# Projection, norm, first routing and its dispatch of a graph and mixture-of-experts kernel put into one block that works by groups of tiles

## What is computed

```python
# graph attention, its last lines: hidden is [2048, 512]
hidden = hidden @ W_out + b_out
x = x + elu(hidden)
# first mixture of experts, on the layer norm of x
h = layernorm(x)
p = softmax(h @ gate_w)                      # 8 experts
w, sel = top_k(p, 2); w = w / w.sum(-1)      # two experts per token
g, u = h @ w_gate[e], h @ w_up[e]            # [512, 384] each
y = (silu(g) * u) @ w_down[e]                # [384, 512]
x = x + sum over the two chosen experts of w * y
```

## Time and profile before

| | us |
|---|---|
| median of 3 runs | 2196.76 (2195.17 to 2202.2) |
| the profiled execution | 2201.98 |
| its span | 2200.2 |
| mean granted TensorE clock | 0.949 |

### The profile page before, as it was taken

The page is one execution under the profiler, slowest core; times in us unless marked ns, Lnnn a source line. Parts: engine busy times, 40 slices in busy tenths (PEclk is TensorE's granted clock), DMA queues, the critical chain, the costliest instruction groups (busy, mean ns, idle before and its releaser), DMA issues. The chain is left out here.

```text
span 2200.2 us, 38541 instructions
## 1 busy us (share of the span) xinstructions
PE 1950.8 (89%) x15937; PEld 1714.8 (78%) x15941; DVE 1280.7 (58%) x1732; ACT 1101.2 (50%) x1182; POOL 468.4 (21%) x335
## 2 busy tenths in 40 slices
PE   4869999999987169999948979949999999999998
PEld 4859999999965069999936857638888888888886
DVE  7799988888656347777758033533434334344342
ACT  4699888886934135555412033224435344253441
POOL 2033222211120422222225401262101011011011
PEclk9979999999989679999979989969999999999999
DMA  6443333323202558888757322253334344353432
GB/s 249 155 164 122 117 108 122 117 83 31 98 6 77 196 183 252 250 250 250 186 168 257 122 77 77 75 150 121 103 119 133 98 134 128 106 138 93 125 104 109
DMA packets 154248, 300.01 MB, mean 136 GB/s; under 512 B 16091, under 2 KB 53083, under 8 KB 149968
## 3 DMA queue, kind: packets, MB, share of 16 engines
q1 hardware_dynamic: 135792, 262.30, 36.9%
q0 software_dynamic: 18336, 35.98, 7.7%
HBM read 227.23 MB, written 79.71 MB: 140 GB/s over the span
## 5 line engine op out<-in xcount | busy, mean ns | idle before, releaser
L823 PE MATMUL attn_acc<-heads_vals,gat_adj 128*128 128x99 bf16 x2048 | 284.6, 209 | 0.0
L2093 DVE TENSOR_TENSOR moe_w_lo<-moe_raw,moe_w_hi 128x2048 fp32r<-128x2048 f32 x64 | 146.8, 2293 | 234.6 <-ACT moe_w_hi L2050 234.6
L821 PE MATMUL attn_acc<-heads_vals,one_x 128*128 128x99 bf16 (+1 forms) x2048 | 240.9, 231 | 18.6 <-DVE one_x L735 13.2
L821 PE MATMUL attn_acc<-heads_vals,heads_mask 128*128 128x99 bf16 (+1 forms) x2048 | 238.5, 229 | 0.0
L2050 ACT CAST moe_w_hi<-moe_raw 128x2048 fp32r<-128x2048 f32 x64 | 122.2, 1909 | 207.8 <-PE moe_y_ps L2018 192.6
L688 ACT ACTIVATE heads_mask<-gat_s_row,heads_big_s 128x2048 fp8e4<-128x2048 f32 x104 | 197.8, 1989 | 35.3 <-PE attn_acc L823 35.3
L821 PEld LDWEIGHTS attn_acc<-heads_vals,one_x 128*128 128x128 fp8e4 x2048 | 197.9, 99 | 15.7 <-issue 15.3
L823 PE MATMUL attn_acc<-heads_vals,attn_below 128*128 128x99 bf16 x2048 | 204.9, 212 | 5.3 <-issue 5.3
L688 ACT ACTIVATE one_x<-gat_s_row,heads_big_s 128x2048 fp8e4<-128x2048 f32 x101 | 192.1, 1989 | 23.5 <-PE attn_acc L823 23.5
L821 PEld LDWEIGHTS attn_acc<-heads_vals,heads_mask 128*128 128x128 fp8e4 x2048 | 197.3, 98 | 5.5 <-issue 5.4
L201 PE MATMUL moe_h_ps<-moe_x_hi,moe_w_hi 128*128 128x512 f32 x512 | 200.1, 391 | 1.6 <-DVE moe_x_lo L2098 1.6
(11 more groups left out here) (347 smaller groups left out, 4736.2 us busy)
## 6 DMA issues: line engine op xcount, KB each, us to landing
moe_raw<-in_L_ffn_W_dram SPq DMA_DIRECT2D x64, 1024.0 KB, 5.2
moe_wg<-in_L_ffn_w_gate_dram SPq DMA_DIRECT2D x23, 768.0 KB, 9.1
moe_wu<-in_L_ffn_w_up_dram SPq DMA_DIRECT2D x23, 768.0 KB, 10.7
moe_wd<-in_L_ffn_w_down_dram SPq DMA_DIRECT2D x23, 768.0 KB, 12.3
gat_s_row<-s_rows SPq DMA_DIRECT2D x16, 1024.0 KB, 6.4
sym_a<-in_adj_dram SPq DMA_DIRECT2D x32, 512.0 KB, 4.3
one_seq<-sent SPq DMA_DIRECT2D x23, 514.0 KB, 3.6
sent<-all_zeros SPq DMA_DIRECT2D x10, 1028.0 KB
```

The costliest lines, as they stand in the source:

```text
L821: mm = pe.matmul(o[:, 0:first], mask[u][:, j, cols], both[:, 0:first], start=(j == 0 and b % 2 == 0), stop=(j == NT - 1), skip_group_check ...
L823: mm = pe.matmul(o[:, 3 * C1:6 * C1], second, both[:, 3 * C1:6 * C1], start=False, stop=(j == NT - 1), skip_group_check=True)
L2093: dve.tensor_tensor(w_lo[n % 2][:], raw[:, n % R], w_hi[n % 2][:], ALU.subtract).then_inc(w_low, 1)
```

## The change

`norm_stats`, `route` and `dispatch_labelled` go; `project_out` becomes `project_route`, one block that holds the projection, the norm, the routing and all 32 indirect transfers. The 16 tiles are taken in five groups (`PASSED`: 4, 4, 4, 2, 2). The main loop has 19 steps; step s multiplies tile s and lets each engine do, at places written out by hand (three per step), the routing work of a group some steps back. The normalizing moves from DVE to ACT and is done twice, into `wide` for the first choice and into a spare region for the second, so that the two copies of a row carry their own weight. The two-buffer `rT_ps` of the routing becomes one buffer, the three-buffer `xT` two.

A token's row in the table no longer depends on the counts of all 16 tiles: expert e owns rows 2048 e and following. So a group can be sent when it is counted. The table grows from 5888 rows to 18176 and is still cleared in whole. The first row of each block of 256 is worked out at the end (`block_row`) and read by SP into a register ahead of each load of rows. The blocks of experts wait for nothing: SP loads rows, then weights.

The diff, cut to its core (setup of tiles and semaphores and the unchanged functions are left out):

```diff
+PASSED = [slice(0, 4), slice(4, 8), slice(8, 12), slice(12, 14), slice(14, 16)]
+PLACES = 3
+PASSED_TURN = [16, 28, 40, 46, 52]
+PASSED_SCORE = [21, 33, 45, 49, 54]
+PASSED_BACK = [22, 34, 46, 50, 55]
+PASSED_RANK = [25, 37, 49, 53, 56]
+CHOOSE_IN = [7, 11, 15, 17, 18]
+PLACE_IN = [8, 12, 16, 17, 18]
+STEPS = NT + 3
...
             def _(pool):
...
+                def send(g, q):
+                    pool.wait_ge(placed, g + 1)
+                    for n in members(PASSED[g]):
+                        row = second(slice(n, n + 1)) if q else wide[:, n:n + 1, 0:ROW]
+                        pool.indirect_dma_start(out=table, ...
...
+                for t in range(NT):
+                    divide(t)
+                    if t == NT - 4:
+                        send(0, 0)
+                    if t == NT - 3:
+                        send(0, 1)
+                for g in range(1, NG):
+                    for q in range(TOPK):
+                        send(g, q)
+                pool.wait_ge(put, SENT)
...
             def _(act):
...
+                for s in range(STEPS):
+                    for g in range(NG):
+                        if s == PASSED[g].stop + 1:
+                            take_root(g)
+                    if 0 <= s - 1 < NT:
+                        exponential(s - 1)
+                    if s + 2 < NT:
+                        high_part(s + 2)
+                    for g in range(NG):
+                        if s == PASSED[g].stop + 1:
+                            normalize(g)
+                    for at in range(PLACES * s, PLACES * s + PLACES):
+                        for g in range(NG):
+                            n = PASSED[g].start + at - PASSED_TURN[g]
+                            if at == PASSED_RANK[g]:
+                                take_tail(g)
+                            if at == PASSED_SCORE[g]:
+                                keep_scores(g)
+                            if n in members(PASSED[g]):
+                                keep_turned(n)
+                    for g in range(NG):
+                        if s == PASSED[g].stop + (2 if g < NG - 1 else 1):
+                            normalize_second(g)
...
             def _(dve):
...
+                for s in range(STEPS):
+                    for g in range(NG):
+                        if s == PASSED[g].stop + 1:
+                            scale(g)
+                    if 0 <= s - 1 < NT:
+                        finish(s - 1)
+                    if s + 2 < NT:
+                        low_part(s + 2)
+                    if 0 <= s - 1 < NT:
+                        take_stats(s - 1)
+                    for g in range(NG):
+                        if s == PASSED[g].stop:
+                            take_variance(g)
+                    for g in range(NG):
+                        if s == CHOOSE_IN[g]:
+                            choose(g)
+                        if s == PLACE_IN[g]:
+                            place(g)
...
             def _(pe):
...
+                def turn_row(n):
+                    pe.wait_ge(normed, n + 1)
+                    if n:
+                        pe.wait_ge(r_copied, n)
...
+                def beside(at):
+                    for g in range(NG):
+                        n = PASSED[g].start + at - PASSED_TURN[g]
+                        if at == PASSED_RANK[g]:
+                            rank(g)
+                        if at == PASSED_BACK[g]:
+                            turn_back(g)
+                        if at == PASSED_SCORE[g]:
+                            score(g)
+                        if n in members(PASSED[g]):
+                            turn_row(n)
...
+                pe.wait_ge(w_loaded, 16)
+                pe.wait_ge(counted, 1)
+                for s in range(STEPS):
+                    if s + 2 < NT:
+                        turn(s + 2)
+                    beside(PLACES * s)
+                    if s < NT:
+                        multiply(s, (0, 1))
+                    beside(PLACES * s + 1)
+                    if s < NT:
+                        multiply(s, (2, 3))
+                    beside(PLACES * s + 2)
...
                 def load_rows(p, r):
+                    row = sp.value_load(block_row[0:1, bass.ds(p, 1)], min_val=0, max_val=table.shape[0] - BR)
                     sp.dma_start(x[:, SB * r:SB * r + SB, :],
-                                 table[bass.ds(p * BR, BR), :].rearrange("(s q) d -> q s d", q=P)).then_inc(x_in[r], 16)
+                                 table[bass.ds(row, BR), :].rearrange("(s q) d -> q s d", q=P)).then_inc(x_in[r], 16)
...
+                load_rows(0, 0)
                 load_weights(0, 0)
+                load_rows(1, 1)
                 load_weights(1, 1)
-                for q in range(TOPK):
-                    for g in range(4):
-                        sp.wait_ge(put[q][g], 64)
-                load_rows(0, 0)
-                load_rows(1, 1)
...
-    rows0, rows1 = NB0 * BR, E * CAP
+    rows0, rows1 = E * N + (NB0 - N * TOPK // BR) * BR, E * CAP
```

More of the change, by code:

```diff
@@ new lines, in project_route @@
+        cmp = c.sb("cmp", [P, E, N // BR])
+        count, blocks, ends = c.sb("count", [P, 1, E]), c.sb("blocks", [P, 1, E]), c.sb("ends", [P, E + 1])
+        cmpb, owned = c.sb("cmpb", [P, NB0, E]), c.sb("owned", [P, NB0, E])
+        blk, skipped, row_at = (c.sb(n, [P, NB0]) for n in ("blk", "skipped", "row_at"))
+        xT = [c.ps(f"xT{u}", [P, KD, P]) for u in range(2)]
+        out = [c.ps(f"out{u}", [P, D]) for u in range(R)]
+        rT_ps = c.ps("rT_ps", [P, KD, P])
+        lgT_ps = c.ps("lgT_ps", [E, G, P])
@@ L901, in project_out, with second, seconds @@
+        put = c.sem("put")
+        def second(tiles):
+            if tiles.start == NT - 1:
+                return last[:]
+            assert tiles.stop < NT
+            return spare[:, ROW * tiles.start:ROW * tiles.stop].rearrange("p (t w) -> p t w", w=ROW)
+        def seconds(g):
+            tiles = PASSED[g]
+            if tiles.stop < NT:
+                return [tiles]
+            return [slice(tiles.start, NT - 1), slice(NT - 1, NT)]
         with nc.Block() as block:
@@ new lines, in scale, with spread @@
+                def scale(g):
+                    tiles = PASSED[g]
+                    dve.wait_ge(rooted, g + 1)
+                    newton_rsqrt(ch, rstd[:, tiles], root[:, tiles], var[:, tiles], tn[:, tiles])
+                    dve.scalar_tensor_tensor(out=shift[:, tiles], in0=mv[:, tiles, 0], scalar=-1.0, in1=rstd[:, tiles],
+                                             op0=ALU.mult, op1=ALU.mult).then_inc(scaled, 1)
+                def spread(row, n):
+                    return row.rearrange("p (a e) -> p a e", a=1).to_broadcast([P, n, E])
@@ new lines, in rank @@
+                def rank(g):
+                    pe.wait_ge(chosen_s, g + 1)
+                    tiles = PASSED[g]
+                    pe.matmul(rank_ps[:, tiles, :], k.before[:], sel[:, tiles, :], start=True, stop=True)
+                    pe.matmul(total_ps[:, tiles, :], k.ones[:], sel[:, tiles, :], start=True, stop=True).then_inc(ranked, 1)
+                def beside(at):
[9 more added lines that the diff above has]
+                            turn_row(n)
```

464 lines of the change are left out of this document (200 added, 264 removed).

## The result

The changed kernel takes 2187.89 us (median of 18 runs, 2183.93 to 2193.89) beside 2198.68 us of the kernel before (18 runs, 2193.53 to 2204.3): the difference of the medians is 10.8 us. The ratio, taken from the runs side by side, is 0.9958, 95% interval 0.995 to 0.9966, so 0.42% faster, about 9.2 us. The profiled execution spans 2190.9 us in place of 2200.2. All medians here are over undisturbed executions; two of the ten of `e3_root_later`, at 3068 and 4640 us, are left out.

The account below looks back on a forecast made before the run. Bound: norm and routing, sends, and first rows and splits end to end. Sum to first expert matmul: 650.2 + 1.9 + 36.9 + 19.5 + 18 + 27.7 + 21.5 = 775.7, against 790.57; median 2181.8 us, range 2164 to 2198.

Parts of the forecast that it names:

- Start: Ahead of tile 0, PE waits for two DVE instructions and turns tile 2 at the slow clock: 1.9 us.
- PE's waits in the loop: In the projection loop PE waits 18 us, mostly for ACT's copies of turned rows queued behind root, exponential and normalizations.
- PE's own work: Projection loop, tiles 5 to 15: 36.9 us plus 19.5 of added turns, scores and ranks, together 56.4 us.
- Rival C: Projection loop: gaps let PE's clock fall, each of three groups paying 3 us; 2191, chance 0.12.
- The tail: From last projection matmul through placing group 2 (7.4 us) and 16 remaining sends on POOL: 27.7 us.
- The start of the experts: After the last send: landing, block change, loading rows and weights, splits, up to the first expert matmul: 21.5 us.
- E: Attention: clears hold back PE's instruction fetch, making the kernel slower; four heads hit give 2215; chance 0.08.
- F: Experts: SP's register read ahead of each row load is not hidden, costing 18 us; 2200, chance 0.03.
- A: Whole kernel: the forecast itself, 2181.8 us, own range 2174 to 2190; chance 0.50.
- Rival B: Projection loop: PE's work covers ACT's list, so the 18 us of waits fall away; 2164, chance 0.20.
- D: ACT: a table change holds it about twice its 1.28 us behind an unfinished instruction, costing 10; 2192, chance 0.04.
- G: Sends: early groups are placed late, so all 32 follow the loop, 20.6 us more; 2202, chance 0.03.

Follow-up runs that it names:

- e3: Changed kernel with ACT's root and DVE's scale moved behind the tile's exponential and the copy for the next tile; 2195.5 us.
- e8: Changed kernel with routing places moved back, all sends behind POOL's divisions, third group's scores kept earlier and two PE waits moved to their use; 2178.2 us.
- e2: Changed kernel with the square root on ACT replaced by a plain copy, so table loads around the roots fall away; 2183.4 us.
- e4: Changed kernel with first weights issued ahead of the wait for the sends, that wait moved into the experts' block, split weights first in memory; 2180.7 us.
- e7: Changed kernel with one more table of 18176 rows cleared beside attention; 2188.9 us.
- e1: Changed kernel with all 32 sends held until the last projection matmul has ended; 2208.7 us.
- e10: e8's loop with its order refined, first weights issued right behind the block change, rows behind the wait for sends, rows split after two weights; 2166.5 us.
- e5: Changed kernel with the places for turning, scoring and ranking a group's rows moved back, a whole step for the first two groups; 2186.2 us.
- e12: e11 with the two small label tiles, 32 bytes, placed ahead of the tile of split rows in memory; 2164.7 us.
- e11: e10 with the first expert's weights issued inside the projection's block; 2167.8 us.
- e9: e8's loop with first weights issued inside the projection's block and the rows split ahead of all three weights; 2176.0 us.

## Why the prediction was right, and where it was off

The sum said 775.7 for the first expert matmul and the trace says 782.97. Of the 15 us of gain 7.6 are there at that point, 9.3 at the end of the span and 10.8 in the medians; the predicted 2181.8 is 6.1 us under the measured 2187.9, inside its range. 1.9 of these 6.1 are the median of the kernel before, 2198.7 over 18 runs in place of 2196.8 over 3. The 7.3 us at the first expert matmul are -0.6 for the start, -3.0 for PE's waits, +5.8 for its work, +1.0 for the tail and +4.1 for the experts' start, so part of the agreement is errors that cancel. Term by term:

- Start, 1.9: real, 1.3. Moving the two waits (e8) shortened PE's wait ahead of tile 0's first multiply from 4.64 to 3.03.
- PE's waits in the loop, 18: 15.0. The size held nearly, the mechanism only in part, so that it held is in part luck. The step that failed is "PE may turn row 2 only behind that copy": PE stood one operation earlier, at the first normalized row (10.4 us; 2.1 for the copies), whose wait the sum had at nothing. Root, table load and exponential are between DVE's variance and it in group 0; in groups 1 and 2 DVE's placing of the group before is as long a chain (e2, e3). The wait for the kept scores in step 15, 2.8, was 2.59.
- PE's own work, 56.4: 62.2. The added work was sized right (three scores of 3.6, rows of 0.35 to 0.6). This is the largest miss. What failed is taking it at full clock: 4.0 of the 5.8 us are the 18 slow projection matmuls behind the waits, some 0.6 more the transposes beside them. Rival C had the mechanism and 9 us for it; it belonged into the sum, at half that size. Two of the three long gaps, and the one of 2.59, lie in stretches of a mean granted clock of 0.72 to 0.77, and the matmuls behind them start 0.43 us apart; the one of 3.37 ending at 682.87 had 1.00 and none. Why that one didn't isn't shown.
- The tail, 27.7: 28.7; 8.45 to the first send of group 2 in place of 7.4, then 16 sends 1.285 apart, as forecast. DVE had placed the group 7.65 us behind the last matmul (736.33), and POOL's send started 0.80 after that, a handoff that the sum had at nothing. Group 4 was placed 2.0 us before POOL got to it, not 3.4, still in time.
- The start of the experts, 21.5: 25.6. Landing and block change were put at 3.3 and took 5.96: the row I took for the block change, 1.4 us from DVE's last instruction to SP, had no sends in front of it, and e4 leaves 4.5 us there without any wait for their landing. Weights 10.2: 11.8. Splits 8.0: 7.9.
- What had to stay hidden: the clears cost nothing (attention's last matmul at 617.7 in place of 617.4, and e7), the register read neither (experts 314.8 us, before 315.6). E and F fell. The 13.3 us a block in the prediction's signs is a slip: it leaves out the experts' last 10 us, and both kernels take 13.7.
- The clock's sign, 1.00 by A and below 0.9 by C, came out between them, at 0.93. Eleven table loads came, five pairs and that of the first exponential, where the prediction counted ten.
- ACT's normalization, bounded by 0.6 and 0.8 and taken at 0.7: four in 2.93 us. The Trainium skill ("ScalarE: Activation LUTs", "What ACT_TABLE_LOAD costs") gives 280 + 0.833 N ns for an operation with one pointer operand, 93 more for the second and 93 of overlap. By it an estimate is 0.80 for one, where the trace's mean is 804 ns, and 0.71 for each next one, 2.93 for four; the trace agrees. It would have settled this bound.
- Rival B (the lists cover each other, 2164) was no property of the change as made. Order alone took the loop from 95.8 us to 88.1 (e8) and 79.7 (e10), but e10 still waits 4.9 us in it, and its 2166.5 has the new start of the experts in it; that B's 18 us can be had in whole isn't shown. D fell: no load lasted over 1.28. G fell; e1 shows a price like its 20.6 us, 20.8 by the medians. That these agree so well is luck: the last send moved by 16.6 us, the span by 16.4.

## What to carry to other kernels

When independent work is laid beside a full engine, read the place of every handoff against the chain that feeds it, not the sum of busy times: here 10.4 us of PE's waiting hung on a few operations standing in front of a link, and moving one place only brought out the next, so all of them had to be moved (first multiply to last: 95.8 us, with e5 92.7, with e8 88.1, with e10 79.7). What a stage boundary costs is to be taken from a boundary with the same work in flight. And a change behind which work starts later gives part of its gain back there; look at what that start can do before the last result is in.

## What the runs showed of the hardware

- Matmuls of gate and up (128x256, split fp32) last 283 to 285 ns on average in the experts' stage when the tiles of rows and weights start a multiple of 64 bytes apart, and 279 to 282 when it is 32 bytes more (e4, e10, e12 against all other kernels); the medians of their weight loads are 192 and 187 to 189 ns. The distances are counted from order and sizes in the code, the traces hold no addresses, and only these two were tried. e12 against e11 moves the rows' tile alone for these matmuls and took 3.3 us off the 23 blocks. The down projection's matmuls don't follow this rule (389 to 393 ns against 393 to 397, see e12).
- Behind indirect sends SP's first issue in the next block came 4.5 and 4.7 us after the last send's end without a wait for their landing (e4, e10), 6.0 to 6.5 with it (changed kernel, e2, e3, e5 to e8), 7.5 behind 32 sends in a row (e1).
- 2.36 MB of weights issued at about the time of the last send delayed the landing of sends: the slowest of the last ones took 6.8 to 7.6 us, in the changed kernel, e8 and e10 3.9 to 4.6, and SP, which waited for it, issued the rows 8.2 to 8.9 us behind the last send's end (e9, e11, e12).
- Writes of zeros beside attention, at a DMA share of 0.92 in place of 0.54, left PE full (29.00 of 29 us, e7) and the time unchanged.
